# A two-block transformer kernel: a new order for its first batch, weights by halves, values in a bank of their own, nine zero products at the head

## The reference

```python
xn = layernorm(x)
s = attn0(xn)         # 16 heads of 16, ALiBi, causal, W_qkv 256x768, W_o
g = silu(ffn0(xn))    # W2 . fwht(silu(xn W1^T) * (xn W3^T)), hidden 1024
x = x + s * g
xn = layernorm(x)
s = attn1(xn)         # 16 heads of 128, RMS norm, rotation, tanh cap, causal
g = silu(moe(xn))     # 16 experts, top 4, and a shared one
return x + s * g
```

## Time and profile before

| | before |
|---|---|
| median of 3 runs | 1235.7 us (1235.22 to 1235.81) |
| the profiled execution, its own time | 1234.86 us |
| its span, first to last instruction | 1233.1 us |
| TensorE busy | 1193.3 us (97%) |
| VectorE, ScalarE, GpSimd busy | 842.9, 601.6, 499.0 us |
| mean granted clock of TensorE | 0.991 of full |
| chain that ended last | PE 89%, issue 3%, DVE 3%, POOL 2%, ACT 1%, DMA 1%, SP's queue 1% |

### The profile page before, as it was taken

The page is one execution under the profiler, slowest core; times in us unless marked ns, Lnnn a source line. Parts: engine busy times, 40 slices in busy tenths (PEclk is TensorE's granted clock), DMA queues, the critical chain, the costliest instruction groups (busy, mean ns, idle before and its releaser), DMA issues.

```text
span 1233.1 us, 26622 instructions
## 1 busy us (share of the span) xinstructions
PE 1193.3 (97%) x9930; PEld 1049.9 (85%) x9930; DVE 842.9 (68%) x1691; ACT 601.6 (49%) x1353; POOL 499.0 (40%) x489
## 2 busy tenths in 40 slices
PE   4999999999999999999999999999999999999997
PEld 3788888888778777777789999999999999999996
DVE  4657777777776344334578788887886667778686
ACT  3444444444434555555555555455545545466443
POOL 1322434443444000000177677766764444444342
PEclk7999999999999999999999999999999999999999
DMA  6745335643667333333311002110010000000001
GB/s 215 244 164 180 133 100 200 215 146 95 242 238 284 95 107 100 108 107 104 120 35 61 26 27 65 31 61 26 27 61 1 35 1 1 1 2 1 1 27 43
DMA packets 65917, 114.93 MB, mean 93 GB/s; under 512 B 7936, under 2 KB 36480, under 8 KB 64384
## 3 DMA queue, kind: packets, MB, share of 16 engines
q1 hardware_dynamic: 59648, 96.45, 23.2%
q0 software_dynamic: 6144, 16.79, 4.3%
HBM read 48.85 MB, written 60.16 MB: 88 GB/s over the span
## 4 chain that ended last, share of the span: by engine, by line
PE 89%; issue 3%; DVE 3%; POOL 2%; ACT 1%; DMA 1%; SPq 1%; POOLq 0%; DVEq 0%; ACTq 0%
PE bank L837 8%; PE six L854 6%; PE bank L916 5%; PE bank L914 5%; PE bank L915 5%; PE six L955 5%; PE bank L464 3%; PE bank L465 3%; PE bank L466 3%; PE bank L992 2%; PE bank L990 2%; PE bank L991 2%; PE bank L927 2%; PE bank L926 2%; PE bank L928 2%
## 5 line engine op out<-in xcount | busy, mean ns | idle before, releaser
L1834 DVE TENSOR_TENSOR sq<-xs 128x512 f32<-128x512 f32 x128 | 131.1, 1024 | 39.3 <-ACT xs L1336 39.3
L2056 POOL TENSOR_TENSOR rstd<-msq,half_pow 128x8 f32<-128x8 f32 x64 | 106.1, 1657 | 95.8 <-DVE msq L1841 94.0
L1317 ACT ACTIVATE pT<-six,rstd 128x256 f32<-128x256 f32 x128 | 60.8, 475 | 169.0 <-PE six L956 169.0
L2068 POOL TENSOR_TENSOR pT<-pT,tri_mul 128x512 f32<-128x512 f32 x64 | 82.0, 1281 | 142.5 <-ACT pT L1365 142.5
L837 PE MATMUL bank<-experts,xT 128*128 x316 | 109.8, 470 | 0.8 <-ACT xT L1261 0.8
L1981 POOL TENSOR_TENSOR hid_l<-hid,hid_h 128x256 fp32r<-128x256 f32 x64 | 50.0, 782 | 149.4 <-ACT hid_h L1092 149.2
L914 PE MATMUL bank<-bw_h,xT1h 128*128 128x512 f32 x256 | 105.6, 413 | 0.8 <-ACT v L1341 0.8
L1405 DVE TENSOR_TENSOR yT1l<-six,yT1h 128x512 fp32r<-128x512 f32 x64 | 44.3, 692 | 84.6 <-ACT yT1h L1370 84.6
L916 PE MATMUL bank<-bw_l,xT1h 128*128 128x512 f32 x256 | 100.3, 392 | 0.0
L915 PE MATMUL bank<-bw_h,xT1l 128*128 128x512 f32 x256 | 99.9, 390 | 0.0
L2059 POOL TENSOR_TENSOR qn<-xs,rstd 128x256 f32<-128x256 f32 x128 | 91.6, 737 | 5.0
(11 more groups left out here) (315 smaller groups left out, 3818.8 us busy)
## 6 DMA issues: line engine op xcount, KB each, us to landing
cells_scratch<-zeros SPq DMA_DIRECT2D x8, 4352.0 KB
xg<-cells_scratch SPq DMA_DIRECT2D x79, 128.0 KB, 2.0
cells_scratch<-y SPq DMA_DIRECT2D x79, 128.0 KB, 1.7
experts<-pack_experts_dram SPq DMA_DIRECT2D x16, 608.0 KB, 10.5
raw<-pack_attn_dram SPq DMA_DIRECT2D x8, 1024.0 KB, 4.9
qkA<-qkc SPq DMA_DIRECT2D x64, 64.0 KB, 2.3
w_full<-pack_w_dram SPq DMA_DIRECT2D x2, 1024.0 KB, 7.2
out_dram<-x_all SPq DMA_DIRECT2D x8, 256.0 KB, 2.1
```

The lines of the kernel that those rows point to most:

```text
L1834: dve.tensor_tensor(out=sq[:, tt, :], in0=x_qk, in1=x_qk, op=ALU.mult).then_inc(sq_sb, 1)
L2056: pool.tensor_tensor(out=rstd[:, r, :], in0=msq[:, r, :], in1=half_pow[:], op=ALU.pow).then_inc(rstd_sb, 1)
```

## The change

The change concerns the head and batch 0 only.

- **Loads.** SyncE now issues `wvo_full` right after the query-key weights, then half 0 of W1 and of W3 (512 KB each), then the two constants, `hadamard` and W2. Only then comes the spread; half 1 of W1 and W3 is issued between its two halves. W3 whole and W2 came after the spread before.
- **Semaphores.** `w1_loaded` and `w3_loaded` become `ffn_loaded[0]` and `ffn_loaded[1]`, one per half; each counts both weights, so the high part of W1's half waits for W3's half too. The small constants move to `x_loaded` and `w2_loaded`.
- **Values.** `values(0)` writes bank 4 of `six` in place of bank 1, and no longer waits for `qk_sb`.
- **Zero products.** `keep_busy` multiplies `nmax`, which is zero then, with itself: six products ahead of the first transposes, three behind them.
- **Order.** On TensorE `up(0, 0)` to `up(0, 2)` come before the first scores, `up(0, 3)` before the second; the four `hadamard_mix` and the later pieces shift. ScalarE and VectorE follow: `vo_hi` and the halves' splits go before and between the two `query_key`, `exps(0, 0)` comes behind the fourth tanh.

Core of the diff:

```diff
+            sp.dma_start(wvo_full[:], pack_vo).then_inc(vo_loaded, 16)
+
+            def load_ffn(n):
+                for full, pack in ((w1_full, pack_w1), (w3_full, pack_w3)):
+                    sp.dma_start(ffn_half(full, n), ffn_half(pack.rearrange("p (k c) -> p k c", k=KD), n))\
+                      .then_inc(ffn_loaded[n], 16)
+
+            load_ffn(0)
             sp.dma_start(stairs32, stairs_c).then_inc(consts_loaded, 16)
             sp.dma_start(kA.rearrange("p g t -> p (g t)"), k_rows_c).then_inc(consts_loaded, 16)
-            sp.dma_start(wvo_full[:], pack_vo).then_inc(vo_loaded, 16)
-            sp.dma_start(w1_full[:].rearrange("p k c -> p (k c)"), pack_w1).then_inc(w1_loaded, 16)
+            sp.dma_start(hadamard[:], hadamard_c).then_inc(w2_loaded, 16)
+            sp.dma_start(w2_a[:], pack_w2).then_inc(w2_loaded, 16)
...
             spread(0, 0)
+            load_ffn(1)
             spread(0, 1)
...
             def first_batch():
+                pe.wait_ge(wa_lo, 5)
+                pe.wait_ge(qk_sb, 2)
+                up(0, 0)
+                up(0, 1)
+                pe.wait_ge(hid_sb, 1)
+                up(0, 2)
                 pe.wait_ge(consts_made, 2)
                 scores(0, 0)
                 maxima_T(0, 0)
                 scores_T(0, 0)
+                pe.wait_ge(hid_sb, 3)
+                up(0, 3)
                 scores(0, 1)
                 mix(0, 0, 0)
-                pe.wait_ge(wa_lo, 6)
-                up(0, 0)
+                pe.wait_ge(fw_lo, 1)
+                hadamard_mix(0)
                 heads_back(0, 0)
                 maxima_T(0, 1)
-                up(0, 1)
                 scores_T(0, 1)
...
+            def keep_busy(n):
+
+                for _ in range(n):
+                    pe.matmul(six[:, 5, 0:T], nmax[:, 0, :], nmax[:].rearrange("p t q -> p (t q)"), start=True, stop=True)
+
+            pe.wait_ge(pow_made, 4)
+            keep_busy(6)
             pe.wait_ge(ident_loaded, 32)
             norm_T0(0)
+            keep_busy(3)
             pe.wait_ge(xT0l_sb, 1)
             pe.wait_ge(wa_lo, 1)
             project(0, 0)
             pe.wait_ge(wa_lo, 2)
             project(0, 1)
-            pe.wait_ge(qk_sb, 2)
             pe.wait_ge(wa_lo, 3)
-            values(0)
+            values(0, six[:, 4, :])
...
             def first_batch():
...
+                hidden(0, 0)
+                hidden(0, 1)
                 maxima(0, 0)
                 queries_max(0, 0)
-                ffn_lo(5, w1_l, w1_full, w1_h, 1)
-                ffn_lo(6, w3_l, w3_full, w3_h, 0)
-                later_consts()
+                hidden(0, 2)
+                hadamard_consts()
+                hadamard_lo()
+                hidden(0, 3)
                 maxima(0, 1)
+                heads_out(0, 0)
+                queries_max(0, 1)
+                ffn_lo(6, w1_l, w1_full, w1_h, 1)
+                down_lo(0)
```

More of the change, by code:

```diff
@@ L212, in build @@
             "x0_loaded", "x_loaded", "later_loaded", "consts_loaded"))
[L213 to L214 removed]
+        ident_loaded, qk_loaded, vo_loaded, w2_loaded = (sem(n) for n in (
+            "ident_loaded", "qk_loaded", "vo_loaded", "w2_loaded"))
+        ffn_loaded = [sem("ffn_half0_loaded"), sem("ffn_half1_loaded")]
         raw_loaded = [sem("raw_loaded0"), sem("raw_loaded1")]
@@ L332, in _ @@
             spread(0, 0)
+            load_ffn(1)
             spread(0, 1)
-            for dst, src in ((hadamard, hadamard_c), (tri_mul, tri_mul_c), (before, before_c)):
-                sp.dma_start(dst[:], src).then_inc(w3_loaded, 16)
-            sp.dma_start(gate_bias[:], gate_b.partition_broadcast(P)).then_inc(w3_loaded, 16)
-            sp.dma_start(w3_full[:].rearrange("p k c -> p (k c)"), pack_w3).then_inc(w3_loaded, 16)
-            sp.dma_start(w2_a[:], pack_w2).then_inc(w2_loaded, 16)
+            for dst, src in ((tri_mul, tri_mul_c), (before, before_c)):
+                sp.dma_start(dst[:], src).then_inc(x_loaded, 16)
+            sp.dma_start(gate_bias[:], gate_b.partition_broadcast(P)).then_inc(x_loaded, 16)
             sp.dma_start(xs_all[:, TT:NT // 2, :],
@@ L635, in project, with values @@
                 last.then_inc(qk0_ps, 1)
-            def values(b):
-                o = banks[1][:, :].rearrange("p (t d) -> p t d", t=TT)
+            def values(b, bank=banks[1][:, :]):
+                o = bank.rearrange("p (t d) -> p t d", t=TT)
                 wv = [w[:, 0:512].rearrange("p (k d) -> p k d", k=KD) for w in (wvo_h, wvo_l)]
@@ L1117, in logits_tanh, with ffn_hi @@
                 act.activation(r_th[:], o[:, :, 0:NE], ACT.Tanh, scale=0.5).then_inc(rth_sb, 1)
-            def ffn_hi(loaded, count, w, full, n):
-                act.wait_ge(loaded, 16 * count)
+            def ffn_hi(w, full, n):
+                act.wait_ge(ffn_loaded[n], 32)
                 act.activation(ffn_half(w, n), ffn_half(full, n), ACT.Copy).then_inc(wa_hi, 1)
@@ L1131, in down_hi, with values @@
                                ACT.Copy, scale=0.25 * float(FF) ** -0.5).then_inc(w2_hi, 1)
-            def values(b, par):
+            def values(b, par, bank=banks[1][:, :]):
                 act.wait_ge(v0_ps, b + 1)
                 after(act, y0_ps, 4 * b)
-                act.activation(v0[:, par, :, :, 0:E0], banks[1][:, :].rearrange("p (t h e) -> p t h e", t=TT, h=H0),
+                act.activation(v0[:, par, :, :, 0:E0], bank.rearrange("p (t h e) -> p t h e", t=TT, h=H0),
                                ACT.Copy).then_inc(v0_sb, 1)
             def first_batch():
-                ffn_hi(w3_loaded, N_W3, w3_h, w3_full, 0)
-                exps(0, 0)
-                ffn_hi(w3_loaded, N_W3, w3_h, w3_full, 1)
-                heads_T(0, 0)
                 gate_tanh(0, 0)
-                hadamard_hi()
                 gate_tanh(0, 1)
                 hidden_hi(0, 0)
+                gate_tanh(0, 2)
+                hidden_hi(0, 1)
+                hadamard_hi()
+                hidden_hi(0, 2)
+                gate_tanh(0, 3)
+                exps(0, 0)
+                hidden_hi(0, 3)
+                heads_T(0, 0)
+                ffn_hi(w1_h, w1_full, 1)
+                down_hi(0)
                 exps(0, 1)
-                hidden_hi(0, 1)
-                gate_tanh(0, 2)
+                ffn_hi(w3_h, w3_full, 1)
+                down_hi(1)
                 heads_T(0, 1)
-                hidden_hi(0, 2)
-                down_hi(0)
+                down_hi(2)
                 exps(0, 2)
-                down_hi(1)
-                down_hi(2)
                 down_hi(3)
-                gate_tanh(0, 3)
+                gate_tanh(0, 4)
                 norm_T0(1)
-                hidden_hi(0, 3)
                 heads_T(0, 2)
                 query_key(1, 0)
-                gate_tanh(0, 4)
+                hidden_hi(0, 4)
+                gate_tanh(0, 5)
                 exps(0, 3)
                 query_key(1, 1)
-                hidden_hi(0, 4)
-                gate_tanh(0, 5)
+                hidden_hi(0, 5)
+                heads_T(0, 3)
                 gate_tanh(0, 6)
-                heads_T(0, 3)
-                hidden_hi(0, 5)
                 hidden_hi(0, 6)
@@ L1220, in _ @@
             norm_T0(0)
+            vo_hi()
+            ffn_hi(w1_h, w1_full, 0)
             query_key(0, 0)
+            ffn_hi(w3_h, w3_full, 0)
             query_key(0, 1)
-            vo_hi()
-            values(0, 0)
-            ffn_hi(w1_loaded, 1, w1_h, w1_full, 0)
-            ffn_hi(w1_loaded, 1, w1_h, w1_full, 1)
+            values(0, 0, six[:, 4, :])
             first_batch()
@@ L1411, in stats @@
                 elif b < NB // 2:
[L1412 removed]
+                    dve.wait_ge(x_loaded, 16 * N_X)
                 else:
@@ L1640, in first_batch @@
                 heads_out(0, 3)
+                hidden(0, 7)
                 maxima(1, 0)
-                hidden(0, 7)
             def batch(b, final):
```

68 lines of the change are left out of this document (27 added, 41 removed).

## The result

The changed kernel takes **1228.2 us**, the median of five executions (1226.06 to 1229.93), beside 1235.7 of the kernel before in the same session (1234.97 to 1235.88). The ratio is 0.9944, with a 95% interval of 0.9933 to 0.9956: 7.5 us less, and nothing overlaps. The forecast was 1231.0 with a range of 1225.3 to 1234.0.

What follows compares the result with a forecast made beforehand. TensorE's idle time (10.2 us) and half-level clock (7.3) were taken as the first batch's loss, 17.5. It falls to 8.2, gain 9.3, less 4.6 for clock falls: 4.7 off 1235.7 gives 1231.0 us, range 1225.3 to 1234.0.

Steps and rivals of the forecast that it cites:

- The head: TensorE up to the projections: nine zero products raise the clock before project(0,0) at 9.39; cost 0, gain 1.3 us.
- Half weights: Loads ahead of the spread: second half weight landed at 11.3 us, up(0,0) starting near 15.2.
- Values in a bank of their own: Values of the first batch no longer wait until bank 1 is read out; the price is nothing.
- The waits: TensorE's idle time in the first batch: seven waits, together 8.2 us in place of 10.2.
- The clock in the gaps: TensorE's clock falls near 22.7 and rises after 6.0 unbroken us: 2.0 and 2.6, together 4.6 us lost.
- a fall in the first gap: Clock falls near 22.7, in the wait after the first scores: 4.6 us lost, gain 4.7; chance 0.34.
- in the second: Clock falls only near 28, before the second scores: 2.6 us lost, gain 6.7, time 1229.0; chance 0.20.
- none: Clock holds through both gaps: gain 9.3, perhaps 10.2 us, time 1226.4 to 1225.5; chance 0.27.
- rival 3: hidden(0,0) on VectorE held up by GpSimd's butterfly, half weights late: 3.4 of 4.7 us gone, 1234.4; chance 0.15.
- Idle 10.2 plus half level 7.3: TensorE's loss in the first 76 us: 10.2 us idle and 7.3 us of half-level clock, 17.5 in all.

Runs made afterwards that it cites:

- sums first: Changed kernel with VectorE's queries_max(0,1) and (0,2) ahead of heads_out (and of batch 1's normalisation): 1241.52 us beside 1251.46 of the kernel before.
- gaps filled: Changed kernel with zero products in its two long waits (4 and 1 around the first transposed maxima, 4 before the second scores): 1225.13 us, kernel before 1234.99.
- filled kernel before: Kernel before, order kept, with zero products at its head and in its three long waits: 1234.65 us beside 1234.99 of the kernel before.
- two filled variants: Kernel before with zero products at head and in waits, 1234.65 us beside 1234.99; the same with exps(0,0) ahead of W3's split, 1253.72 beside 1254.64.
- nearly identical kernel: Changed kernel with VectorE's queries_max ahead of heads_out in two places: ratio 0.9923 (0.9910 to 0.9937) to the kernel before.
- all three together: Changed kernel with zero products in its two gaps, exps(0,0) before the fourth tanh and queries_max first: 1239.65 us beside 1251.46 of the kernel before.

## Why the prediction was right, and where it was not

**The head.** "Six of them ... delay nothing, cost 0, gain 1.3." They held TensorE from 2.08 to 7.36, 0.88 for a product and not the 0.77 that I took, and `project` started 0.34 late (in six other traces the same products took less, 4.25 to 5.27 in place of 5.49). The clock was up as forecast, and the projections ended 1.0 sooner instead of 1.3. But hardly any of it reaches the end: without the zero products `up(0, 0)` starts only 0.3 later, since W3's half sets its start. "Gain 1.3" is right as an entry of the sum, whose other side is the wait of 1.3 before `up(0, 0)`, and wrong as the price of the zero products.

**Half weights.** Forecast: landed at 11.3, `up(0, 0)` at 15.2. Measured: ScalarE copied the first at 11.33, `up(0, 0)` started at 15.18. The working that asked how many KB lie ahead in the list was good to 0.1 us.

**Values in a bank of their own.** "The price is nothing" was read as no cost, and I put no gain beside it. The gain was inside my 1.3 us wait before `up(0, 0)`, which the old bank would have made about 1.8 us longer. I never worked out that case: the step is silent on the part of the change that was worth 1.8 us at `up(0, 0)` in the trace.

**The waits.** Forecast 1.3, 1.9, 0.5, 1.9, 0.7, 0.7, 1.2, in all 8.2. Measured 0.87, 1.95, 0.52, 1.97, 0.74, 0.42, 0.98, in all 7.45. Nothing I had not listed turned up. A walk through the lists with durations from the trace of before gave seven waits to within 0.45 us each.

**The clock in the gaps** is the term that was mis-sized. I took a fall near 22.7 that costs 4.6 us. In the profiled execution it fell at 25.1 for 3.4 us and cost 1.3. That is the fastest of five, and the only one with a trace; of the others span and mean granted clock are on record. The clocks, fastest first, are 0.998, 0.997, 0.997, 0.996, 0.993 at 1226.06, 1228.0, 1228.2, 1229.19 and 1229.93 us. The lower the clock, the longer the time, which fits a clock that stays down for longer but doesn't show it to be all. The median stands 2.1 us above the profiled one, so if the clock is all that differs, the term is 1.3 + 2.1 = 3.4 us in the median and 5.2 in the slowest. The forecast's 4.6 is inside what happens and 1.2 too much for the median. Those 1.2, the 0.75 of shorter waits, and the two short waits behind 76 us (0.8) that I had not counted, less the 0.34 at the head, make 2.4 of the 2.8 us between 1231.0 and 1228.2. What I had as three cases with chances (a fall in the first gap, in the second, none) turned out to vary between executions and close variants: the traces show a fall at the end of the first gap (without the zero products and with the sums first, at 23.2 and 23.3), falls between the two gaps (24.7, 25.1, 25.3, and 27.4 with the values in bank 1), none at the second gap, and, with the gaps filled, none there. That the forecast came within 2.8 us with this term taken from a single row is in part luck. The rule of the Trainium skill that I had cited (TensorE: Matmul & The Clock Gate, "Why this matters for your kernels") warns only of longer gaps, and the traces do not bear it out as a limit: the clock fell with 1.95 us of idle time, two transposes and 0.52 more behind it.

**Another wait (rival 3)** did not come. VectorE did `hidden(0, 0)` in 0.42 and 0.42 us in the middle of GpSimd's butterfly:

```profile
15.64 4.75 POOL L1990 TENSOR_TENSOR x_all<-w_a 128x1024 f32<-128x1024 f32 x2 [9.72 <-DMA w_a<-pack_w_dram]
```

```profile
17.42 0.42 DVE L1483 SCALAR_TENSOR_TENSOR th<-th,bank 128x256 f32<-128x256 f32 x1 [2.30 <-ACT th L1102]
17.87 0.42 DVE L1487 TENSOR_TENSOR hid<-bank,th 128x256 f32<-128x256 f32 x1
```

The rule of the Trainium skill on the shared port pair (SBUF — State Buffer, "Who interferes with whom"), that a VectorE instruction with at most one input in SBUF and outside the two-port modes doesn't contend with GpSimd, held here: each of the two reads one of its inputs from a bank.

**The bookkeeping itself.** "Idle 10.2 plus half level 7.3" is the right size for a loss, and the wrong list of what can be had singly. The filled kernel before removed most of the second item and got 0.3 us (1.0 by the spans). Each item was hidden behind another: the slow clock behind W3's load, ScalarE's order behind VectorE's. What the change got right is to move all of them at once. Which share of the 7.5 us is the loads' and which the new lists' was not tried; an early `up(0, 0)` needs both, since W3 arrives at 27 with the old loads, and the old list has `up(0, 0)` behind the second scores. The runs show only that at `up(0, 0)` the zero products bring 0.3 and the bank 1.8, and that the clock, alone or with ScalarE's order, brings nothing that is told apart from noise on the old loads.

**What I had not priced at all:** with W2 loaded early the butterflies moved from under VectorE's constants, and these moved down its list. `gate_bias` takes 0.15 us, at 38.4, where the kernel before and its two filled variants have 2.16 to 2.18, in front of `maxima(0, 1)`.

## What to carry to other kernels

Before you price a lost microsecond, ask what would stop TensorE next if it were back: a slow clock in front of a late load costs next to nothing, and filling the waits shows that cheaply. Walk the new instruction lists engine by engine with durations from the old trace; here that gave each wait to within half a microsecond. Once loads and order are right, the gaps that are left are where the clock falls, and there zero products pay, but only where TensorE really waits: one filling too many cost 1.9 us, and the next change of order can turn a good filling into such a one.

## What the runs showed of the hardware

The fall of the clock is not the same from one execution to the next of one program: the changed kernel's two traces, with the same waits, have one fall (at 25.1) and two (at 25.3 and 45.8), the second with TensorE busy without a break since 44.7. Behind the same gap of 1.95 and 0.52 us it stayed at half for 3.4 us in one trace and for 13.6 us in a nearly identical kernel's, up to 36.9, though TensorE was busy for 4.99 of the 5.60 us from 23.4 on. Nor is it up again only at work: it rose at 28.5, in an idle time. Two waits before `up(0, 0)` of nearly one length give one trace in which the level falls (1.83, all three together) and one in which it doesn't (2.09, gaps filled).

VectorE and GpSimd seem to hold each other up; the pairs are read from the traces, and no run takes one apart. `gate_bias`, a 128x16 operation from SBUF to SBUF, takes 2.16 us under the butterfly and 0.15 without it. The other way round, `hid_l` on GpSimd takes 2.53 us at 25.32 while VectorE subtracts for `had_l` (24.98, 2.29), beside 0.76 on average later.

The same kernel before took 1235.0, 1251.5 and 1254.6 us in three sessions; the first two ran on the same chip, so another chip isn't what makes the step of 16. In the changed kernel's trace of the third, 17.5 of the 19.1 us arose behind batch 2's start. Some 13 of them are waits of TensorE that the first trace doesn't have: 3.9 in all before the transposes of the later batches, released by VectorE's `hid`, and one of 6.1 near the experts, are the largest. The clock was also at half from 397.4 to 404.2. What makes the waits is open. The first batch's waits are alike in both traces.
